# A fused attention and FFN kernel on one core: the first FFN's down-projections of eight chunks as blocks of seven products

## The reference, cut to what matters

```python
# x: 8 x 128 x 512, that is 1024 tokens of 512
x = x + attn(cond(x))             # cond: a linear layer with gated low-rank experts
x = x + ffn(cond2(x))             # ffn: three linear layers with low-rank updates
# in attn, besides seven small products ("orders"), stands the FIRST FFN, F = 1248:
ffn_out = silu(h @ ffn_gate_w.T) * (h @ ffn_up_w.T) @ ffn_down_w.T
return approx_out + ffn_out
```

## Time and profile before

| what | value |
|---|---|
| median of 3 runs | 452.35 us (451.96 to 453.01) |
| profiled execution, time | 452.02 us |
| its span, first to last instruction | 450.3 us |
| busy: PE, DVE, ACT, POOL | 446.6 (99%), 287.5 (64%), 196.2 (44%), 38.2 (8%) us |
| instructions | 5498, of them 2033 recorded matmuls |
| DMA | 41.22 MB, mean 92 GB/s |
| granted TensorE clock | 1.000 |

### The profile page before, as it was taken

One profiled execution on the slowest core, in us unless ns is written; L12 is line 12 of the kernel. 1 busy time (PEld: TensorE's weight loads), 2 busy tenths in 40 slices (PEclk: granted clock), 3 DMA queues, 4 the chain that ended last, 5 costly groups with the idle time before them and its releaser, 6 DMA issues.

```text
span 450.3 us, 5498 instructions
## 1 busy us (share of the span) xinstructions
PE 446.6 (99%) x2033; PEld 368.8 (82%) x2033; DVE 287.5 (64%) x415; ACT 196.2 (44%) x302; POOL 38.2 (8%) x57
## 2 busy tenths in 40 slices
PE   9999999999999999999999999999999999999997
PEld 7788888888888888888888888888888888888886
DVE  5756699655655345566676246989863468897631
ACT  6364442345553124656444337465641124665300
POOL 1004210252100121210000000000000000000000
DMA  8407730138721777670531010122101132122022
GB/s 283 147 0 219 186 58 1 51 100 177 183 39 47 223 142 170 154 166 25 170 111 47 17 45 3 64 79 58 55 34 26 68 95 64 47 53 65 1 97 89
DMA packets 21866, 41.22 MB, mean 92 GB/s; under 512 B 2704, under 2 KB 5536, under 8 KB 21840
## 3 DMA queue, kind: packets, MB, share of 16 engines
q1 hardware_dynamic: 16416, 32.25, 22.5%
q0 software_dynamic: 5424, 8.63, 11.1%
...
## 4 chain that ended last, share of the span: by engine, by line
PE 99%; DVE 0%; issue 0%
PE PS L1316 18%; PE PS L1317 18%; PE PS L1318 18%; PE PS L1454 13%; PE PS L1455 13%; PE PS L1453 13%; PE PS L1541 1%; PE PS L1379 1%; PE PS L1330 0%; PE PS L1600 0%; PE PS L1611 0%; PE PS L1610 0%; PE PS L1554 0%; PE PS L1328 0%; PE PS L1598 0%; PE PS L1562 0%
## 5 line engine op out<-in xcount | busy, mean ns | idle before, releaser
L1454 PE MATMUL PS<-HT,WU 128*128 128x512 f32 x266 | 103.6, 389 | 0.0
L1453 PE MATMUL PS<-HT,WU 128*128 128x512 f32 x266 | 103.6, 389 | 0.0
L1455 PE MATMUL PS<-HT,WU 128*128 128x512 f32 x266 | 103.5, 389 | 0.0
L1455 PEld LDWEIGHTS PS<-HT,WU 128*128 128x128 f32 x266 | 49.9, 188 | 10.4
L1453 PEld LDWEIGHTS PS<-HT,WU 128*128 128x128 f32 x266 | 50.0, 188 | 10.3
L1454 PEld LDWEIGHTS PS<-HT,WU 128*128 128x128 f32 x266 | 50.0, 188 | 10.2
L431 ACT ACTIVATE WU<-raw 128x256 fp32r<-128x256 f32 (+2 forms) x48 | 42.0, 883 | 33.4 <-DMA raw<-raw 12.4
L811 DVE TENSOR_TENSOR WU<-raw,WU 128x256 fp32r<-128x256 f32 (+2 forms) x49 | 48.5, 996 | 12.0 <-ACT WU L431 11.6
L811 DVE TENSOR_TENSOR G<-T,G 128x1024 fp32r<-128x1024 f32 (+1 forms) x33 | 33.7, 1030 | 27.8 <-ACT G L431 27.3
L431 ACT ACTIVATE PS<-PS 128x512 f32<-128x512 f32 x38 | 22.1, 583 | 58.9 <-PE PS L1455 58.1
L1316 PE MATMUL PS<-G,DW 128*128 128x512 f32 (+1 forms) x122 | 47.1, 386 | 0.0
...
## 6 DMA issues: line engine op xcount, KB each, us to landing
raw<-in_pieces SPq DMA_DIRECT2D x87, 256.0 KB, 2.9
...
raw<-raw POOLq DMA_DIRECT2D x10, 256.0 KB, 4.8
X<-in_x SPq DMA_DIRECT2D x8, 256.0 KB, 5.4
out_x<-X SPq DMA_DIRECT2D x7, 256.0 KB, 2.1
...
```

What stands on the lines that cost most here:

```text
L1453: pe.matmul(bank, w[:, 1, cols], xx[:, 0, :], start=start and kc == 0, stop=False, skip_group_check=not start)
L1454: pe.matmul(bank, w[:, 0, cols], xx[:, 1, :], start=False, stop=False, skip_group_check=not start)
L1455: mm = pe.matmul(bank, w[:, 0, cols], xx[:, 0, :], start=False, stop=kc == 1, skip_group_check=not start)
```

## The change

- The first FFN becomes one chain of 14 blocks of seven products: u0 u1 u2 u3 d0 d1 u4 u5 u6 u7 d2 d3 u8 u9 (u: gate and up of a chunk; d: down-projection). q counts them from 0 to 13. d0 and d1 do the down-projection of chunks 0 to 3 for output rows 0 to 255 and 256 to 511, d2 and d3 that of chunks 4 to 7. Chunks 8 and 9 keep the classic form (`tail`).
- The weights of all 14 blocks, the down blocks' too, get their four sums by the DMAs described above.
- The moving side of a down block is g of four chunks, with its own T1 to T4: `g_sum` (one DVE addition after an even chunk, two after an odd one) and `g_sum4`. g is split in parts as they come: event 0 after the even chunk; events 1 (T2 and one more), 2 (B21 and B22) and 3 (T4) after the odd chunk. Before, it was one split of 1024 columns for each chunk.
- Down blocks end in `x_out` a, b, c, d: four DVE additions onto X. `half_step` and `pass_add` of the first FFN are gone.
- Before u3 and u7 end, p1 of the next block isn't taken ahead; `enter_down` orders p1(q), p5(q), p1(q+1), p6, p2, p7, p3, p4.
- POOL loads `lora_b` after all sums, not between chunks 1 and 2. G has 14 slots, DW is the last two of them; banks are renamed. ACT's and DVE's order of the next stage's preparation changes: a2 before x1(0), the last S2 piece after x1(0).

TensorE's work: 420 matmuls for gate and up as before; down 4 x 42 + 48 = 216 instead of 240. The second FFN is the same but for names.

```diff
+BLOCKS = [("u", 0), ("u", 1), ("u", 2), ("u", 3), ("d", 0), ("d", 1), ("u", 4), ("u", 5), ("u", 6), ("u", 7),
+          ("d", 2), ("d", 3), ("u", 8), ("u", 9)]
+TAIL = 8
...
-                if p in P_CHUNK[0]:
-                    c = P_CHUNK[0].index(p)
-                    if prior_sums(c):
-                        sp.wait_ge(w_ready, P_CHUNK[0][prior_sums(c)[-1]] + 2)
-                    sp.dma_start(sum_region(c), parts[c][:, 0:1024]).then_inc(sum_in[par(0, c)], 16)
+                if p in P_BLOCK:
+                    q = P_BLOCK.index(p)
+                    if q > 1:
+                        sp.wait_ge(w_ready, P_BLOCK[q - 2] + 2)
+                    sp.dma_start(sum_region(q), parts[q][:, 0:1024]).then_inc(sum_in[q % 2], 16)
...
+            def steady1(q):
+                part1_hi1(q + 1, p4_done, q)
+                copy_bc1(q, *c_free(q - 1))
+                g_first(q)
+                copy_e1(q)
+                g_later(q, 2)
+                part2_hi1(q + 1)
+                silu1(q, 0)
+                g_later(q, 3)
+                next_a(q)
+                silu1(q, 1)
+            def enter_down(q):
+                copy_ab1(q, *b_free(q - 2))
+                part1_hi1(q + 1, p4_done, q)
+                g_first(q)
+                copy_e1(q)
+                g_later(q, 2)
+                copy_ab1(q + 1, *b_free(q - 1))
+                copy_bc1(q, *c_free(q - 1))
+                part2_hi1(q + 1)
+                g_later(q, 3)
...
+            def block1(q):
+                up = is_up(q - 1)
+                c = number(q - 1) if up else None
+                pair = up and c < TAIL and c % 2
+                if first_down(q):
+                    g_sum(c)
+                    mul0_1(c)
+                    part1_lo1(q + 1)
+                    g_lo1(c, 1)
+                    g_lo1(c, 2)
+                    g_sum4(c)
+                    add_b1(q)
+                    g_lo1(c, 3)
...
+                if not is_up(q):
+                    x_out(q, "a")
+                add_d1(q)
+                if pair and not first_down(q):
+                    g_lo1(c, 3)
+                part2_lo1(q + 1)
+                if is_up(q):
+                    mul1_1(number(q))
+                else:
+                    x_out(q, "d")
+                    x_out(q, "b")
...
+            for k in range(3):
+                s2_lo(k)
+            for h in range(HALVES):
+                dve.wait_ge(hi_lora, h + 1)
+                lo(a2_part(h, 1), a2_raw(h), a2_part(h, 0)).then_inc(lora_ready, 1)
+            x1(0)
+            s2_lo(3)
```

More of the change, by code:

```diff
@@ new lines, in b_free, with c_free, event, g_count @@
+        def b_free(q):
+            return (silu[1], number(q) + 1) if is_up(q) else (out_b, number(q) + 1)
+        def c_free(q):
+            return (g_mul[0], number(q) + 1) if is_up(q) else (out_c, number(q) + 1)
+        def event(c, e):
+            return 2 * TAIL + 2 * (c - TAIL) + e if c >= TAIL else 4 * (c // 2) + e
+        def g_count(c):
+            return 2 * TAIL + 2 * (C1 - TAIL) + c + 1
+        def g_op(c, op):
+            return G[:, 2 * op + c // 2 % 2]
+        def g_ops(c, op, step, part):
+            a = 2 * op + c // 2 % 2
+            return G[:, a:a + 2 * step + 1:2 * step, part, :]
@@ L557, in full_hi @@
                 if j == 2:
[L558 to L567 removed]
+                    act.wait_ge(p4_done, fast(1, 9) + 1)
@@ new lines, in tail, with seven2, moving @@
+            def tail(h, j):
+                c = TAIL + j
+                pe.wait_ge(w_ready, P_TAIL + j + 1)
+                pe.wait_ge(g_ready, event(c, h) + 1)
+                for o in range(KC):
+                    mm = product(PB[DOWNB[h][o]], tail_w(j), tail_g(c, h), chunk(o), j == 0, c == C1 - 1)
+                    if c == C1 - 1:
+                        mm.then_inc(down1_done, 1)
+            def seven2(c, weight, op, bank, start):
+                def moving(kc):
+                    return HT[:, op, kc, 0, :], HT[:, op, kc, 1, :]
+                return seven(WU[:, wu_set(c)], weight, par(c), moving, PB[bank], start)
```

1117 lines of the change are left out of this document (638 added, 479 removed).

## The result

| | before | after |
|---|---|---|
| median | 452.68 us (451.96 to 454.26, 4 runs, one more than above) | 459.19 us (458.84 to 459.42, 4 runs) |
| profiled execution: time, span | 452.02, 450.3 us | 459.42, 457.4 us |
| busy PE, DVE, ACT, POOL | 446.6, 287.5, 196.2, 38.2 us | 446.7, 317.0, 211.7, 46.4 us |
| instructions; recorded matmuls | 5498; 2033 | 5562; 2009 |

The ratio is 1.0133, 95% interval 1.0113 to 1.0154: slower by 1.3%. The forecast was 461.0 (454.5 to 465.5).

The account below looks back on a forecast made before the run. PE was taken to bound the kernel, with the DMA-made sums nearly late. From 452.02 us, minus 5.4 for fewer matmuls, plus 9.6 first-FFN and 4.5 next-stage waits gave 460.7, stated as 461.0; range 454.5 to 465.5.

Parts of the forecast that it names:

- C: First FFN: time from SP's 512 KB issue to ACT's part2_hi; 16.37 us in the first round, 16.2 in five others.
- Part 1: Fewer matmuls in the first FFN's down-projections: 24 fewer at 0.227 us take 5.4 us off PE's path.
- Part 2: First FFN: late sums and in-order work make PE wait 9.6 us, at blocks 3, 4, 9, 10 and 13.
- The lower bound: First FFN: with C at 13.3 only in-order engine work makes PE wait, 5.1 us, near 1.8 per down-block entry.
- the ring: First FFN: one weight set's repeating round of DMA-made sums, 19.3 to 20.0 us against PE's 19.04, longer after the change.
- The even set isn't last: First FFN: weight sets of even blocks have only plain rounds and start 9.5 later, so they don't set PE's waits.
- The signs: Profile rows expected if right: PE waits at blocks 3, 4, 9, 10, 13 and base, part2_hi waiting, PE busy well below 99%.
- Part 3: Down blocks: the extra VectorE work of x_out costs nothing, except x_out a at the entries.
- Part 4: Next stage: PE's base waits 4.5 us for its fourth bank, freed by x1(1) behind the split of W2's fourth piece.
- The rival of the clock: PE's waits bring its clock down to 1.2 GHz; 466 us and more, chance 0.05 shared with longer transfers.
- The easing ring: First FFN: C falls below 14.1 as waits thin transfers, leaving only in-order waits; 453.2 to 456.2 us, chance 0.13.
- Faster: At each down-block entry g's last part is ready in time, so waits total 2.0 us; 450.1 us, chance 0.10.

Follow-up runs that it names:

- kernel 8: Changed kernel with SP's load of a block's sums held until the previous block's sums landed, so two chains never overlap; 484.6 us, one run.
- kernel 1: Changed kernel with g's last split no longer ahead of the split of the sums, in blocks 2 and 8 and at the down-block entries; 456.9 us.
- kernel 2: Changed kernel with only the next stage's preparation reordered (splits, x1 additions, ScalarE's high copies); 453.7 us.
- kernel 3: Changed kernel with the edits of kernel 1 and kernel 2 together; 452.2 us.
- kernel 4: Changed kernel with nine extra matmuls, results overwritten, filling PE's wait at the fourth bank of base; 458.2 us.
- kernel 6: Kernel 1 with the two DMA additions of each block's sums cut from 128 partitions to 16, the other sums left out; 453.3 us.
- kernel 11: Kernel 7 with nine repeated splits of a W2 piece ahead of the x1(1) additions, making PE stand at base; 456.8 us.
- kernel 7: Kernel 3 with the last addition of the sums made by VectorE instead of a DMA for blocks 4 to 8 and 10 to 13; 449.6 us.
- kernel 9: Kernel 7 with VectorE's last addition behind add_b in blocks 3 and 9, and part1_hi and part1_lo moved earlier at down-block entries; 449.9 us.

## Why the prediction was right, and where not

The sum was 452.0 - 5.4 + 9.6 + 4.5 = 460.7. The profiled run of after gives 452.0 - 5.4 + 7.1 + 5.7 = 459.4. Two terms were off by 2.5 and 1.2 us on opposite sides, so part of the nearness to 461.0 is luck; with either one put right the other error alone gives 458.2 or 461.9, both still in the range. (Its end "457.5 with C at 15.7" is 457.7 by its own sum.)

- **Part 1**, 24 matmuls by 0.227: exact, as the books close on it.
- **Part 2, the places.** They are where the forecast had them, but for block 13; the sizes aren't. Block 3 took 1.26 us with the matmul behind it (forecast 0.8), p4 of block 4 1.1 (near 2) behind 0.84 in small waits (0.8), block 10 0.9 and 0.85 (the same), block 9 0.6 (near 2) and block 13 nothing (0.5 by its sum). Block 7 and the blocks behind the entries took 1.0 that the list had not named. The step that failed is "for the other five I take C = 16.2". The ends of the odd set were forecast at 145.4, 164.9, 186.0, 207.9, 227.4 and came at 145.0, 164.6, 184.2, 205.5, 223.2: near while C was near 16, too late from q = 9 on.
- **Why C wasn't a constant.** C = 16.0 to 16.7 in before was the price of a chain with the other set's transfers beside it: its last addition issued at 186.23 has SP's next load at 186.44. Alone C is 12.8 to 13.5 (kernel 8). Each wait of PE moves the sets against each other, so C changes from round to round and from kernel to kernel: 13.4 to 16.8 in after, 18.8 in kernel 1. The forecast's reason for 16.2 was a next load some 8 us behind this set's own. It came 8.2 us behind for q = 5, 7, 9 and 11, and C was still anything from 14.5 to 16.3, so that distance alone doesn't set it. The lower bound, 5.1 us for the in-order work alone, was the best number of the prediction: 5.35 measured with the additions cut short, and 1.8 for each entry in both. The 4.5 above it were forecast as the ring, and were 1.7.
- **"The even set isn't last"** held in after and not in kernels 1 to 4: a stand at p5 of block 4 in kernels 1 and 3, and one of 0.94 us at p1 of block 5 in kernels 2 and 4, which have after's own first FFN. That it held was in part the luck of the run.
- **The signs.** Those at blocks 3, 4, 9 and 10 and the one at `base` came. Three did not: no wait at block 13, no wait of `part2_hi` in blocks 11 and 13, and PE's busy share fell only to 98%, since part of each wait and the slow matmuls count as busy. Of the signs of being wrong, C below 14 came once.
- **Part 3**, `x_out`: nothing, as said, but for its part in the entries.
- **Part 4.** T, the end of block 13, is 232.88. The fourth S2 copy came at T + 6.3 (forecast 7.5), the split of W2's fourth piece ended at T + 18.1 (19.2), and the bank was free at T + 18.7 (19.9). The mechanism is the forecast's, 1.2 us sooner. Against the 14.8 without waits this is 3.9 us (4.5 forecast). Of the 1.8 us above it 1.6 were matmuls at 1.2 GHz.
- **The rival of the clock** had a chance of 0.05 and a price of 5 and more. It came in small: PE stood 2.05 us at the bank, some 1.4 us after it went on the level fell, and seven matmuls took 0.427 us each (the forecast had twice 0.227), two more something between. The rivals were not exclusive; a fall of the clock should have stood in the term of Part 4 as a surcharge of 0 to 2 us. The Trainium skill, "TensorE: Matmul & The Clock Gate", Part 1, says that an idle PE is put to half clock: the rows of after and of kernels 4, 6 and 11 agree.
- **The easing ring** was half right: C fell under 14.1, its condition, in one round (13.37).
- **"Faster", 450.1**, isn't what this change does, but its time is what kernel 7 reaches, with g's last split, the last addition and the next stage's order mended: 449.6 is 2.9 us under the kernel before, measured beside it. The rest of the 5.4 is in the 3.0 us of waits still left; kernel 9 tried for them and got nothing, so that they can be had isn't shown.
